# A transformer block on one core: rows of x per partition, the columns' DMA queue, a shorter PE warm-up, and the order of low parts

## The reference

```python
mod = (_silu(L0_c) @ L0_wmod).reshape(L0_c.shape[0], 6, 1, -1)
sa, ca, ga, sb, cb, gb = (mod[:, i] for i in range(6))   # ga, gb: floored at 0.25 in size
h = _layernorm(x) * (1 + ca) + sa
Q, K, V = jnp.split(h @ c_attn_w + c_attn_b, 3, axis=2)
base_A = softmax(Q[:, :, :128] @ K[:, :, :128].T * SCALE)
cam_bias = tanh((base_A @ V[:, :, :128]) * cam_gate) @ K[:, :, :128].T * (SCALE * layer_weight)
x = x + ga * (softmax(Q @ K.T * SCALE + cam_bias) @ V @ c_proj_w + c_proj_b)
h = _layernorm(x) * (1 + cb) + sb
x = x + gb * (gelu(h @ proj1.T + proj1_bias) @ proj2.T + proj2_bias)
```

## Time and profile before

| what | us |
|---|---|
| median of 3 runs | 322.08 |
| lowest, highest | 321.79, 323.62 |
| the profiled execution's own time | 322.67 |
| its span in the profile | 320.9 |
| PE busy | 313.8 (98%) |
| DVE, ACT, POOL busy | 214.3, 157.6, 108.5 |

### The profile page before, as it was taken

One profiled execution on the slowest core, in us unless ns is written; L12 is line 12 of the kernel. 1 busy time (PEld: TensorE's weight loads), 2 busy tenths in 40 slices (PEclk: granted clock), 3 DMA queues, 4 the chain that ended last, 5 costly groups with the idle time before them and its releaser, 6 DMA issues.

```text
span 320.9 us, 5227 instructions
## 1 busy us (share of the span) xinstructions
PE 313.8 (98%) x2022; PEld 283.9 (88%) x2022; DVE 214.3 (67%) x415; ACT 157.6 (49%) x266; POOL 108.5 (34%) x131
## 2 busy tenths in 40 slices
PE   8889999999999999999999999999999999999996
PEld 6778989888999998898899888898999999899895
DVE  5695689996555669886743789898664575753531
ACT  2465575563334337816932486545532244860930
POOL 4431755154445656135011132140021232603311
PEclk9999999999999999999999999999999999999999
DMA  7920030600000000000001000000000000001001
GB/s 219 375 64 1 0 67 1 239 24 0 3 0 2 0 2 1 2 33 33 3 22 43 2 1 2 0 2 0 0 2 0 2 0 2 0 3 50 16 7 62
DMA packets 8025, 10.31 MB, mean 32 GB/s; under 512 B 704, under 2 KB 6592, under 8 KB 8000
## 3 DMA queue, kind: packets, MB, share of 16 engines
q1 hardware_dynamic: 8000, 9.98, 9.4%
HBM read 7.35 MB, written 2.10 MB: 29 GB/s over the span
## 4 chain that ended last, share of the span: by engine, by line
PE 86%; DVE 9%; ACT 3%; issue 2%; DVEq 0%
PE a_ps L190 13%; PE a_ps L189 13%; PE a_ps L188 13%; PE s_ps L188 11%; PE s_ps L190 11%; PE s_ps L189 11%; PE t_ps L1096 7%; DVE nmax L750 2%; PE s_ps L938 2%; PE t_ps L1023 2%; DVE k_lo L720 1%; PE s_ps L953 1%; DVE th L732 1%; DVE q_hi L718 1%; ACT prob L524 1%
## 5 line engine op out<-in xcount | busy, mean ns | idle before, releaser
L514 ACT ACTIVATE pt_hi<-t_ps 128x512 fp32r<-128x512 f32 x64 | 35.0, 596 | 67.6 <-PE t_ps L1096 67.5
L750 DVE TENSOR_REDUCE nmax<-s_ps 128x1 f32<-128x1024 f32 x32 | 39.0, 1220 | 14.9 <-PE s_ps L190 14.9
L524 ACT ACTIVATE prob<-s_ps,nmax 128x1024 f32<-128x1024 f32 x32 | 35.8, 1119 | 13.3 <-DVE nmax L750 13.1
L744 DVE TENSOR_TENSOR pt_lo<-t_ps,pt_hi 128x512 fp32r<-128x512 f32 x64 | 40.9, 681 | 1.3 <-ACT pt_hi L514 1.3
L188 PE MATMUL s_ps<-k_hi,q_hi 128*128 128x512 f32 x96 | 38.4, 400 | 0.2 <-DVE k_lo L671 0.2
L344 POOL TENSOR_SCALAR prob<-prob,rinv 128x1024 f32<-128x1024 f32 x16 | 18.0, 1127 | 58.3 <-DVE rinv L754 58.3
L190 PE MATMUL s_ps<-k_hi,q_lo 128*128 128x512 f32 x96 | 37.7, 393 | 0.0
L189 PE MATMUL s_ps<-k_lo,q_hi 128*128 128x512 f32 x96 | 37.5, 391 | 0.0
L188 PE MATMUL a_ps<-v_hi,pt_hi 128*128 128x256 f32 x128 | 36.8, 288 | 0.0
L188 PE MATMUL a_ps<-w_hi,pt_hi 128*128 128x256 f32 x128 | 36.4, 284 | 0.0
L189 PE MATMUL a_ps<-w_lo,pt_hi 128*128 128x256 f32 x128 | 36.2, 283 | 0.0
(11 more groups left out here) (150 smaller groups left out, 760.6 us busy)
## 6 DMA issues: line engine op xcount, KB each, us to landing
w_raw<-w_t SPq DMA_DIRECT2D x2, 1024.0 KB, 6.2
out<-x_all SPq DMA_DIRECT2D x16, 128.0 KB, 1.7
x_all<-x SPq DMA_DIRECT2D x4, 256.0 KB, 4.8
wmod_raw<-wmod SPq DMA_DIRECT2D x1, 1024.0 KB, 8.5
x_all<-x SPq DMA_DIRECT2D x2, 512.0 KB, 10.3
wmod_raw<-wmod SPq DMA_DIRECT2D x1, 512.0 KB, 4.8
wattn_raw<-w_attn SPq DMA_DIRECT2D x1, 512.0 KB, 6.0
gates<-h SPq DMA_DIRECT2D x4, 128.0 KB, 2.6
```

What stands on the lines that cost most here:

```text
L514: A(pt_hi[:, (u // 2) % 2, 4 * g:4 * g + 4, (u % 2) * P:(u % 2 + 1) * P], t_bank(b, "p", 2 * u + g)[:, :].rearrange("p (t n) -> p t n", n= ...
L524: A(prob[:, u % 3, :], s_ps[u % 2][:, :], ACT.Exp, bias=nmax[:, u:u + 1], accum_out=rsum[:, u:u + 1]).then_inc(exp_ready, 1)
L744: V.tensor_tensor(pt_lo[dst], t_bank(b, "p", 2 * u + g)[:, :].rearrange("p (t n) -> p t n", n=P), f(pt_hi[dst]), ALU.subtract).then_inc(pt ...
L750: V.tensor_reduce(nmax[:, u:u + 1], s_ps[u % 2][:, :], AX.X, ALU.max, negate=True).then_inc(nmax_ready, 1)
```

## The change

Four edits. First, the layout of x and of the output: a partition holds eight neighbouring tokens of a batch (token 8p + t in partition p, tile t), where it held every 128th (token 128t + p). A load of two tiles is then one run of 2 KB in each partition, and no longer two runs of 1 KB; a store of a tile is 1 KB a partition as before, with 8 KB from one partition's run to the next. Second, the loads' order: the columns go to ACT's queue, and the third and fourth x loads ahead of `wvt` and `wp`. Third, four zero matmuls in place of nine, and the zeroed tile is 256 columns wide and no longer 512. Fourth, on ACT and DVE the affine of the second half comes ahead of the high part of V's tile 1 and of the low parts of k (job 1) and V's tile 1.

```diff
-    x_v = x.rearrange("b (t p) e -> p (b t) e", p=P)
-    out_v = out.rearrange("b (t p) e -> p (b t) e", p=P)
+    x_v = x.rearrange("b (p t) e -> p b t e", p=P)
+    out_v = out.rearrange("b (p t) e -> p b t e", p=P)
...
-            load_x(0, 0, 2)
-            sp.dma_start(cols_sb[:, :], cols).then_inc(cols_in, 16)
-            load_x(1, 2, 2)
+            load_x(0, 0, 0, 2)
+            load_x(1, 0, 2, 2)
             sp.dma_start(wmod1_raw[:, :, :], wm[:, :, 0:2 * E]).then_inc(wmod1_in, 16)
             sp.dma_start(wattn_raw[:, :, 0:2 * E], wa[:, :, 0:2 * E]).then_inc(wqk_in, 16)
+            load_x(2, 0, 4, 2)
+            load_x(3, 0, 6, 2)
             sp.dma_start(wvt_raw[:, :, :], wv_t.rearrange("(c p) n -> p c n", p=P)).then_inc(wvt_in, 16)
             sp.dma_start(wp_raw[:, :, :], wp.rearrange("(c p) n -> p c n", p=P)).then_inc(wp_in, 16)
-            load_x(2, 4, 2)
-            load_x(3, 6, 2)
...
+            act.dma_start(cols_sb[:, :], cols).then_inc(cols_in, 16)
             act.wait_ge(cols_in, 16)
...
-            v_high(0, 1)
             h_high(3)
             h_high(2)
+            v_high(0, 1)
             v_high(0, 2)
...
-            V.memset(f32s[:, 0, :], 0.0).then_inc(warm_ready, 1)
+            V.memset(f32s[:, 0, 0:2 * P], 0.0).then_inc(warm_ready, 1)
...
             qk_low(0)
             v_low(0, 0)
-            qk_low(1)
-            v_low(0, 1)
             h_full(2)
             h_full(3)
             h_low(3)
             h_low(2)
+            v_low(0, 1)
             v_low(0, 2)
+            qk_low(1)
...
-            warm_up(9)
+            warm_up(4)
```

More of the change, by code:

```diff
@@ L260, in _, with load_x @@
         def _(sp):
-            def load_x(i, t, n):
-                sp.dma_start(x_all[:, t:t + n, :], x_v[:, t:t + n, :]).then_inc(x_in[i], 16)
+            def load_x(i, b, t, n):
+                sp.dma_start(x_all[:, b * T + t:b * T + t + n, :], x_v[:, b, t:t + n, :]).then_inc(x_in[i], 16)
             wa = w_attn.rearrange("(c p) n -> p c n", p=P)
             wm = wmod.rearrange("(c p) n -> p c n", p=P)
-            load_x(0, 0, 2)
-            sp.dma_start(cols_sb[:, :], cols).then_inc(cols_in, 16)
-            load_x(1, 2, 2)
+            load_x(0, 0, 0, 2)
+            load_x(1, 0, 2, 2)
             sp.dma_start(wmod1_raw[:, :, :], wm[:, :, 0:2 * E]).then_inc(wmod1_in, 16)
             sp.dma_start(wattn_raw[:, :, 0:2 * E], wa[:, :, 0:2 * E]).then_inc(wqk_in, 16)
+            load_x(2, 0, 4, 2)
+            load_x(3, 0, 6, 2)
             sp.dma_start(wvt_raw[:, :, :], wv_t.rearrange("(c p) n -> p c n", p=P)).then_inc(wvt_in, 16)
             sp.dma_start(wp_raw[:, :, :], wp.rearrange("(c p) n -> p c n", p=P)).then_inc(wp_in, 16)
-            load_x(2, 4, 2)
-            load_x(3, 6, 2)
             sp.dma_start(wattn_raw[:, :, 2 * E:3 * E], wa[:, :, 2 * E:3 * E]).then_inc(wv_in, 16)
@@ L279, in _ @@
                 .then_inc(rows_in, 16)
-            load_x(4, T, TH)
-            load_x(5, T + TH, TH)
+            load_x(4, 1, 0, TH)
+            load_x(5, 1, TH, TH)
             sp.wait_ge(gate_floor, 2)
@@ L294, in _ @@
                     wait(sp, y_ready, b, t + 1)
-                    sp.dma_start(out_v[:, b * T + t, :], x_all[:, b * T + t, :]).then_inc(y_out, 16)
+                    sp.dma_start(out_v[:, b, t, :], x_all[:, b * T + t, :]).then_inc(y_out, 16)
             sp.wait_ge(y_out, 16 * B * T)
```

## The result

The changed kernel takes **325.87 us**, the median of 12 runs (324.31 to 327.25); the kernel before, in 12 runs of its own (321.79 to 326.55), takes 323.16 us. The ratio is 1.0081, with a 95% interval of 1.0055 to 1.0107: slower by 0.8%. The forecast was 320.1 with a range up to 323.8. The profiled execution took 326.15, its span is 324.3, 3.4 more than before.

The account below looks back on a forecast made before the run. It took PE's pace from its first scores matmul (26.20 us) as the bound. From 322.67, 1.9 for (a) and 0.77 for (b) gave 320.0, or 319.4 for a slow profiled run; it took 320.1, range 319.4 to 323.8.

Parts of the forecast that it names:

- What bounds it: PE paces the 295 us from its first scores matmul (26.20); time saved ahead of that comes off the end one for one.
- (a): At the start: four zero matmuls for nine, new loads and layout bring modulation and transposes earlier; 1.9 us, bounds 1.5 to 2.3.
- the load at 6.0: Modulation's weights (wmod) land at 6.0 us, between ends of 5.05 and 6.45, so modulation starts 2.0 us earlier.
- lands at 6.45 at the latest: The wmod load, issued about 0.5 us earlier on SP, was to land no later than 6.45, against 6.97 before.
- 188 against 365 GB/s: Load rates at 3 to 4 and 5 to 6 us; 2 KB x pieces at the higher rate would save 1.4 us.
- R1: Rival: PE's clock stays low after the shorter warm-up; mild form 321.5 to 323 us, chance 0.15; full form 0.2.
- R1's full form: Clock low through modulation, transposes and the first half's projections and fold, 4.0 us more: 323.7 to 326.6 us, chance 0.2.
- (b): Second half's affine on DVE and ACT ahead of low parts: ACT's second ht_hi 0.77 us earlier, bounds 0 to 1.07.
- R2: Rival: 2 KB pieces no faster, or wp or wqk late; (a) gives only 1.0, time 320.9; chance 0.15 with R3.
- R3: Rival: (b) gives nothing because another low part is late in its place; time 320.8; chance 0.15 together with R2.
- (c): The 16 output stores with rows in new order: only the last is seen, charged nothing, bounds 0.3 us either way.
- the 0.59 of excess: Profiled run's 322.67 us over the median 322.08; already in the sum if from the zero matmuls' late end, else 319.4.

Follow-up runs that it names:

- e2: The kernel before with four zero matmuls for nine and nothing else: 325.72 us, ratio 1.0097.
- e5: The kernel before with only the new order of ACT's high parts and DVE's low parts: 322.27 us, ratio 1.0008.
- e6: The kernel before with the new order and two more zero matmuls between first transposes and first projection: 322.13 us, ratio 0.9984.
- e9: e6 with seven zero matmuls at the start for nine: 321.08 us, ratio 0.9979 to the kernel before.
- e12: The kernel before with the columns' load behind wmod on SP's own queue: 326.75 us, ratio 1.0136.
- e3: The kernel before with only the new layout of x and of the output: 323.21 us, ratio 1.0034.
- e13: e10 with the new layout of x and output: 322.58 us, ratio 0.9991 to the kernel before.
- e4: The kernel before with only the columns' load on ACT's queue: 322.75 us, ratio 1.0007.
- e8: The changed kernel with the old layout of x and output, four zero matmuls kept: 326.62 us, ratio 1.0129 to the kernel before.
- e14: e10 with the columns' load on ACT's queue: 322.23 us, ratio 0.9986 to the kernel before.
- e1: The changed kernel with nine zero matmuls again: 323.03 us, ratio 1.0011 to the kernel before.
- e7: The changed kernel with nine zero matmuls and two more between first transposes and first projection: 321.95 us, ratio 0.9987 to the kernel before.
- e11: The kernel before with two zero matmuls between first transposes and first projection, without the new order: 322.14 us, ratio 0.9998.
- e10: e6 with eight zero matmuls at the start for nine: 321.51 us, ratio 0.9976 to the kernel before.

## Why the prediction was wrong

**What bounds it** was right: after the first `scores` 294.8 us passed, 294.7 before, and a microsecond lost ahead of it was a microsecond lost.

**(a), the load at 6.0: wrong, beyond its own bound.** I put the latest landing at 6.45, by taking the 0.5 of an earlier issue as 0.5 of an earlier landing, and hoped for more from longer pieces. It landed at 7.65. The first step that failed is "lands at 6.45 at the latest", and with it the term of 1.9, which measured 0.31. With the old layout and the columns on SP's queue `wmod` took 4.3 to 5.1 from issue, in eight profiles (the kernel before, e2, e5, e6, e9 to e12); with the 2 KB pieces alone it took 5.9 and 5.6 (e3, e13), with the second queue alone 5.9, 6.2 and 5.9 (e4, e8, e14), with both 6.0, 5.7 and 6.5 (the changed kernel, e1, e7). So each of the two edits by itself makes it later by more than the scatter, and e12 shows no gain from the earlier issue. I read 188 against 365 GB/s as the effect of the piece's size, while the stretch stays slow with either size (135 to 185 GB/s from 2 to 4 us after the change). The Trainium skill, DMA: Bandwidth & Descriptors, "Specifications", names 512 B as the least size for line rate. That agrees with this slow stretch in so far as it is no quicker with 2 KB pieces; that they would make the load later, the passage does not say.

**R1, the clock: the case that came, at 0.2.** Its mechanism, a low clock in modulation and behind it, and its first prices were right: modulation plus 1.73 (1.68 forecast), transposes plus 0.88 (0.94), then the projections. It stayed low through L953 and L957 and came back at 17.6, ahead of nearly all of the fold, so 1.57 of the 4.0 were paid, more than the 1.1 from which slower begins. The second step that failed, and the larger, is that the sum charged nothing for the clock, with R1's full form at a chance of 0.2; it cost 4.18. I counted the spread of the runs against the trace's 5.0 us of work, and with an idle time of 1.2 us; it was 3.1, since the load was late. The two faults thus fed each other in the changed kernel's profile: the clock did rise in the block and was lost while PE waited for the load. But e2 shows that the shorter warm-up is enough by itself: the wait is 1.6 there, the clock had not risen, and the time is 325.7. The trace of before had shown no rise before 5.0 us of work, and that row should have weighed more than the scatter, though it is no bound either: the changed kernel's seventh record, 2.7 us after its first, already took 494 ns, and its last 380.

The account closes: the profiled 326.15 is 6.15 above the sum's 320.0, of which 4.18 are the low clock, 1.59 what (a) fell short, 0.18 what (b) fell short, and 0.2 lie behind the first `scores` and in rounding. That 326.6, the end of R1's full form, came within 0.5 of it is luck: it was made of 6.6 us of low clock and the whole of (a). And 320.1 lies above both sums that it was drawn from, 320.0 and 319.4.

**R2** was right that the pieces are no faster and wrong on the price: its 1.0 for (a) took `wmod` to land as before, it landed 0.7 later and (a) gave 0.31, and it left out the clock. `wp` was in time: no wait before L1005. **R3** did not come.

**(b): right, a little oversized.** 0.77 forecast (0.79 by its own rows, 20.53 to 21.32), 0.59 in the changed kernel, 0.63 in e5, and 0.58 between e11 and e10 (14.63 and 14.05 from the first projection to `scores`). DVE's idle time before `k_lo`, of which a quarter of a microsecond was to be left, is 0.43. ACT's second `ht_hi` followed the first without idle time, as expected (the two stand in one row):

```profile
23.21 0.81 DVE L656 TENSOR_SCALAR h<-t_ps,modc 128x512 f32<-128x512 f32 x1
...
23.64 1.45 ACT L482 ACTIVATE ht_hi<-t_ps,modc 128x512 fp32r<-128x512 f32 x2 [0.53 <-PE t_ps L1023]
...
24.63 0.81 DVE L656 TENSOR_SCALAR h<-t_ps,modc 128x512 f32<-128x512 f32 x1 [0.61 <-ACT ht_hi L482]
...
26.82 0.19 PEld L962 LDWEIGHTS s_ps<-ht_lo,wqk_hi 128*128 128x128 f32 x1 [0.41 <-DVE ht_lo L663]
```

What is missing lies where the bounds had put it: DVE's second `h` waited 0.61 for ACT's first copy, so `ht_lo` gained less, and the weight load of L962 waited for it.

**(c)** the store: 1.9 us to landing for 1.7, within the bound.

**The baseline.** The median of three that I was given was 322.08; over twelve runs in that job it is 323.16, with four of them at 324.7 to 326.6, and in the later jobs 322.4 to 322.6. I took the 0.59 of excess in the profiled execution as a late end of the zero matmuls. The later traces agree in kind: the same nine end at 7.1 in e6 and at 7.7 in e5, and at 8.2 in the kernel before.

## What to carry to other kernels

A warm-up of TensorE is not idle work to be cut to the length of the wait it fills: it has to reach the clock's rise in every execution and to join up with real work. So cut it by measuring many executions, and look at the highest of them and at each one's mean granted clock as well as at the median. A mean of 1.000 beside a long time is a warning too, since the reading is 1.00 before the first rise. Before taking cover away from a load, see in the trace when it lands with the new order of issues; an issue moved up by half a microsecond is no landing moved up by as much. When a stretch of tiny matmuls and transposes stands between warm-up and work, a filler in a gap on PE can keep the clock more often, at no cost where PE would have waited anyway (e1 against e7: seven falls of twelve, and one).

## What the runs showed of the hardware

- The granted clock fell from 1.00 to 0.50 in a wait of 3.1 us without PE work (changed kernel, at 7.5). It also fell with PE shown busy for most of the time: at 8.7, 0.8 us after PE had come back from a wait of 3.0 (e8); at 10.8, after a wait of 1.4, modulation and transposes (e7); and at 11.2, 12.3 and 11.4, after a wait of 0.5, modulation, transposes and a gap of 1 us (e1, e3, e4). It came back in the midst of the projections, at 17.6 in the changed kernel and before 15 in e1.
- The moment of the first rise moves from execution to execution. The first zero matmul of 379 or 380 ns starts at 4.2 in the changed kernel, between 4.5 and 5.8 in e1, e4, e5, e6, e9, e10 and e13, and at 6.7 in the kernel before; in e2 and e8, with eight records up to 4.6 and 4.3, there is none.
- The granted clock reads 1.00 while the durations are those of the lower level, up to the first rise (e2: 353 ns a record at 6.8 to 10.0, against 352 in the changed kernel at a reading of 0.50).
- 128 pieces of 2 KB at a pitch of 8 KB in memory are no quicker than 256 of 1 KB: DVE started on the second x load 4.8 and 4.5 us after its issue (e3, 1.61 to 6.44; e13, 1.63 to 6.12), with the old layout 3.2 to 3.6 us after (e5, e9, e10, e11, each of which waited for it).
- With an 11 KB load on a second queue, beside the first 512 KB of the other, `wmod` took 5.9 to 6.2 us from issue in place of 4.3 to 5.1 (e4, e8, e14). What in the queues does this was not tried, nor was the columns' load on ACT's queue at a later time.
